# Ten loads of weights and constants move from SyncE's queue to GpSimd's, spread over tiles 0 to 5

## The reference

```python
xn = layernorm(x)
# linear attention, 16 heads of 32
Q = elu(xn @ wq.T + bq) + 1;  K = elu(xn @ wk.T + bk) + 1;  V = xn @ wv.T + bv
KV = einsum('bhsd,bhse->bhde', K, V)
out = einsum('bhsd,bhde->bhse', Q, KV) / (Q . sum_s(K) + 1e-8)
attn = out @ wo.T + bo
# gated FFN (512 -> 1376 -> 512) with a shared LoRA and 8 routed LoRA experts, top 2
gate, up = xn @ W_gate + lora + expert_lora, xn @ W_up + lora + expert_lora
ffn = (silu(gate) * up) @ W_down + lora + expert_lora
return x + attn + ffn
```

## Time and profile before

| What | Value |
|---|---|
| median of 3 runs | 675.92 us (674.55 to 676.27) |
| profiled execution: its own time | 675.29 us |
| profiled execution: span of the records | 673.5 us |
| TensorE busy | 661.8 us, 98% of the span |
| VectorE, ScalarE, GpSimd busy | 375.6, 256.3 and 126.9 us |
| granted TensorE clock | 1.00 |

### The profile page before, as it was taken

How to read it: one execution, slowest core, us unless ns; L and a number is a source line. 1 busy time by engine, 2 the same in 40 slices (tenths; PEclk the granted TensorE clock), 3 DMA queues, 4 the chain that set the end, 5 groups by cost and what they waited for, 6 DMA issues and landing times.

```text
span 673.5 us, 10336 instructions
## 1 busy us (share of the span) xinstructions
PE 661.8 (98%) x3568; PEld 544.2 (81%) x3568; DVE 375.6 (56%) x696; ACT 256.3 (38%) x412; POOL 126.9 (19%) x290
## 2 busy tenths in 40 slices
PE   7999999999999999999999999999999999999998
PEld 6889899977677788888888888888888888888886
DVE  5577788778775966344346433445444336534433
ACT  4343445467235324323233332333233314323321
POOL 3456666635256130000000000000000000000000
PEclk9999999999999999999999999999999999999999
DMA  7946566753853679940024100012400002300001
GB/s 222 328 158 225 194 202 203 249 213 150 307 218 115 253 242 3 43 161 0 0 79 169 82 0 0 0 63 78 187 0 0 0 0 78 126 0 0 0 0 62
DMA packets 40634, 74.21 MB, mean 110 GB/s; under 512 B 19280, under 2 KB 19920, under 8 KB 38688
## 3 DMA queue, kind: packets, MB, share of 16 engines
q1 hardware_dynamic: 40400, 73.56, 37.5%
q0 software_dynamic: 208, 0.30, 0.4%
HBM read 52.81 MB, written 21.04 MB: 110 GB/s over the span
## 4 chain that ended last, share of the span: by engine, by line
PE 89%; DVE 4%; issue 2%; ACT 1%; POOL 1%; DMA 1%; SPq 0%; POOLq 0%; DVEq 0%; ACTq 0%
PE bank L1196 20%; PE bank L1197 19%; PE bank L1198 19%; PE bank L1438 18%; PE bank L1411 6%; PE bank L1424 2%; DVE den L1049 1%; PE bank L1422 1%; DMA w_raw<-in_wkT 1%; PE bank L1213 1%; PE bank L1225 1%; PE bank L1311 1%; DVE qf_odd L1007 1%; PE bank L1449 1%; PE bank L1451 1%
## 5 line engine op out<-in xcount | busy, mean ns | idle before, releaser
L1196 PE MATMUL bank<-x,up_h 128*128 128x512 f32 (+1 forms) x352 | 137.1, 390 | 0.2 <-DVE x3r L1014 0.2
L1197 PE MATMUL bank<-x,up_h 128*128 128x512 f32 (+1 forms) x352 | 137.2, 390 | 0.0
L1198 PE MATMUL bank<-x,up_l 128*128 128x512 f32 (+1 forms) x352 | 137.1, 390 | 0.0
L1139 DVE TENSOR_TENSOR hf<-bank,silu 128x512 f32<-128x512 f32 x44 | 30.4, 691 | 155.4 <-issue 135.6
L1438 PE MATMUL bank<-dn,hid_h 128*128 128x512 f32 x352 | 108.7, 390 | 0.0
L660 ACT ACTIVATE hid_h<-hf 128x512 fp32r<-128x512 f32 x44 | 27.8, 632 | 142.4 <-DVE hf L1139 142.4
L1196 PEld LDWEIGHTS bank<-x,up_h 128*128 128x128 f32 x352 | 66.1, 188 | 16.5 <-issue 0.7
L1438 PEld LDWEIGHTS bank<-dn,hid_h 128*128 128x128 f32 x352 | 65.9, 188 | 14.7 <-DVE res L1158 0.6
L1197 PEld LDWEIGHTS bank<-x,up_h 128*128 128x128 f32 x352 | 66.1, 188 | 14.2
L1198 PEld LDWEIGHTS bank<-x,up_l 128*128 128x128 f32 x352 | 66.1, 188 | 13.8
L849 DVE TENSOR_TENSOR up_l<-up_raw,up_h 128x1024 fp32r<-128x1024 f32 x44 | 55.0, 1249 | 26.9 <-ACT up_h L660 26.9
(11 more groups left out here) (165 smaller groups left out, 1081.7 us busy)
## 6 DMA issues: line engine op xcount, KB each, us to landing
x<-scr_x SPq DMA_DIRECT2D x7, 2048.0 KB, 9.3
up_raw<-in_ffn_up SPq DMA_DIRECT2D x11, 768.0 KB, 7.9
scr_x<-xt SPq DMA_DIRECT2D x16, 512.0 KB, 5.3
xin<-in_x SPq DMA_DIRECT2D x16, 256.0 KB, 4.6
scr_z<-zt SPq DMA_DIRECT2D x16, 256.0 KB, 2.0
x3r<-in_x SPq DMA_DIRECT2D x16, 256.0 KB, 3.5
scr_att<-x3r SPq DMA_DIRECT2D x16, 256.0 KB, 2.7
z<-scr_z SPq DMA_DIRECT2D x4, 1024.0 KB, 4.9
```

The costliest lines, as they stand in the source:

```text
L1139: nc.vector.tensor_tensor(hf[:], ps_u[:], silu[:], ALU.mult).then_inc(h_done, 1)
L1196: nc.tensor.matmul(dst, lh, rh, start=start, stop=False, **kw)
L1197: nc.tensor.matmul(dst, lh, rl, start=False, stop=False, **kw)
L1198: return nc.tensor.matmul(dst, ll, rh, start=False, stop=stop, **kw)
```

## The change

SyncE's part loses the ten loads and the wait for `wsetl_done`. GpSimd's loop over 13 tiles becomes six written-out tiles with loads between them, and a loop from tile 6 on. There is one load behind tile 0, one behind tile 1, and two behind each of tiles 2 to 5. The sizes, the destinations, the count on `s2_in` and the wait in tile 8 stay.

```diff
@@ sync
             stage1(0, 0)
 
-            for dst, name in ((hmask, "headmask"), (hcol, "headcol"), (hrow_raw, "headrow"), (lomask, "lomask"), (bdn_raw, "b_dn"), (sb_dn, "sb_dn")):
-                sp.dma_start(dst[:], dram[name]).then_inc(s2_in, 16)
-            sp.dma_start(bv_b[:], dram["bv"]).then_inc(s2_in, 16)
-            sp.dma_start(bo_b[:], dram["bo"].to_broadcast([P, D])).then_inc(s2_in, 16)
-            sp.wait_ge(wsetl_done, 2 * KD)
-            sp.dma_start(w_raw[:, 0], dram["woT"]).then_inc(s2_in, 16)
-            sp.dma_start(w_raw[:, 1], dram["wqT"]).then_inc(s2_in, 16)
@@ gpsimd
             rstd_of(1)
             rstd_of(2)
-            with pool.Fori(0, TILES - 3) as t:
+            def load(dst, src):
+                pool.dma_start(dst, src).then_inc(s2_in, 16)
+
+            route(0)
+            pool.wait_ge(wsetl_done, 2 * KD)
+            load(w_raw[:, 1], dram["wqT"])
+            route(1)
+            load(w_raw[:, 0], dram["woT"])
+            route(2)
+            load(hmask[:], dram["headmask"])
+            load(hcol[:], dram["headcol"])
+            route(3)
+            load(bv_b[:], dram["bv"])
+            load(hrow_raw[:], dram["headrow"])
+            route(4)
+            load(lomask[:], dram["lomask"])
+            load(bdn_raw[:], dram["b_dn"])
+            route(5)
+            load(sb_dn[:], dram["sb_dn"])
+            load(bo_b[:], dram["bo"].to_broadcast([P, D]))
+            with pool.Fori(6, TILES - 3) as t:
                 route(t)
             route(TILES - 3, more=False)
```

## The result

The changed kernel takes 679.19 us (median of 7 runs, 676.93 to 680.45) against 674.94 us (7 runs, 674.55 to 676.27) for the one before: ratio 1.0054, 95% interval 1.0043 to 1.0066. By the ratio it is slower by 3.6 us (the two medians lie 4.25 us apart), where I had forecast 1.5 us faster, and it lies 0.8 us above my range.

What follows compares the result with a forecast made beforehand. TensorE was taken to bound the kernel, busy 661.8 us, 98% of the span. The terms -2.32 + 0.7 + 0.1 gave -1.5 us, so 675.92 - 1.5 = 674.4 us, range 673.2 to 678.4 us.

Steps and rivals of the forecast that it cites:

- The gain: Ten loads off SyncE's queue: tile 1's store lands earlier, ScalarE's stall in tile 3 goes, at most 2.32 us saved.
- GpSimd's lag: GpSimd issuing two loads in each of tiles 2 to 5 lengthens its tiles; 0.7 us lost after hidden time.
- c: GpSimd's added time per load between a tile's last operation and the next `rden1`; taken as 0.60 us, bounds 0.54 to 1.47.
- 4 (2c - 0.65) - 1.5: Loss in us from GpSimd's issuing over tiles 2 to 5, less a lead; 0.7 us at c = 0.60.
- the lead: How far `zst` is ready ahead of TensorE once the stall is gone; estimated 1.5 us, set against GpSimd's lag.
- the 0.65 us: Free time per tile: TensorE's 7.54 us a tile against a 6.89 us loop through GpSimd, VectorE and back.
- The round trip: From one tile's `rden1` through VectorE and GpSimd to the next tile's `rden1` and hand-over; 6.89 us without loads.
- the rival that I feared most: GpSimd is held longer per load than its queue shows, deciding at c = 0.80; 675.9 to 681.3 us, chance 0.27.
- the third, "the DMA engines": Moved 3.3 MB share the DMA engines with the stores of tiles 2 to 8; 0.1 us lost, bounds 0 and 0.6.
- the whole slack: Slack from a store to TensorE's next keys, put at 0.7 to 1.5 us, about as large as that of `zst`.
- the moved loads delay later stores: Rival: a store in tiles 4 to 8 lands 1 to 2.6 us late, ScalarE waits; 676.2 us, chance 0.10.
- The constants' wait: Wait in tile 8: the last load, issued at about 70, lands before wq is split at 78 to 80; costs nothing.

Runs made afterwards that it cites:

- act_issue: Kernel before, with the ten loads issued by ScalarE on its own queue at the end of its tiles 1 to 6; 673.10 us, ratio 0.9968.
- the two tiny kernels: sp_late and act_issue, each with ten extra 512-byte transfers issued by GpSimd at the changed kernel's places; 676.22 us and 674.14 us.
- sp_spread: Kernel before, with all ten loads still on SyncE but spread behind the stores of tiles 2 to 7; 673.19 us, ratio 0.9971.
- after_again: The changed kernel itself, measured once more; 679.96 us, ratio 1.0063 to the kernel before.
- sp_late: Kernel before, with all ten loads on SyncE in one block behind the store of tile 2; 674.92 us, ratio 0.9994.
- after_bo_plain: Changed kernel, with `bo_b` loaded from an ordinary array of 128 rows instead of one row read 128 times; 677.16 us, ratio 1.0037.
- pool_constants2: act_issue, with the eight constants issued by GpSimd and the two weights left on ScalarE; 677.06 us, ratio 1.0026 to the kernel before.
- after_last_act: Changed kernel, with the last pair, `sb_dn` and `bo_b`, issued by ScalarE behind its tile 6; 675.39 us, ratio 1.0003 to the kernel before.
- after_swap: Changed kernel, with its last two pairs of loads swapped, so `lomask` and `bdn_raw` come last; 676.37 us, ratio 1.0009 to the kernel before.
- pool_weights2: act_issue, with the two weights issued by GpSimd and the eight constants left on ScalarE; 674.50 us, ratio 0.9989 to the kernel before.
- unrolled_only: Kernel before, with GpSimd's first six tiles written out and no load moved; 674.82 us, ratio 0.9993.

## Why the prediction was wrong

**The gain** was right: -2.32 us forecast; 2.32 in those two tiles of the changed kernel, and 2.25 us of stage 1 in act_issue, where nothing takes it away. The profile looked as I had said, no wait in tile 3 and full tiles of 7.99 and 7.09 us.

**GpSimd's lag** came out about right, in part by luck: +0.7 us forecast, 0.5 to 0.6 us in stage 1 and 1.4 us by the times of the two tiny kernels. c is 0.49 (0.60 forecast), far from the 0.80 at which it would have decided, and with it the formula, 4 (2c - 0.65) - 1.5, gives -0.2, so nothing: c was too high, and the lead or the 0.65 us too large. The round trip itself was right: over two loads it is 7.8 us a tile (`rden` of the changed kernel at 55.02, 62.83 and 70.65), and 6.89 + 2 x 0.49 gives 7.87. So the rival that I feared most, with 0.27, did not come. The 1 us that the Trainium skill's page DMA: Bandwidth & Descriptors (Latency and other measured facts) gives to the first byte is not time for which GpSimd is held. As a latency this trace agrees with it better than the earlier trace rows: `sb_dn` is issued at 69.48, and the software queue's first packets are seen between 70.5 and 71.

**The step that failed is the third, "the DMA engines": 0.1 us, with 0.6 as its upper bound.** Measured, what the moved data does is 4.4 to 5.0 us (5.8 to 6.4 us of loss against act_issue, less the 1.4 us of the issues), 3.4 to 4.1 us of it by the last pair alone. What the term left out is that transfers on GpSimd's queue keep SyncE's store from landing for far longer than their bytes take. It went wrong in three ways.
- I read the room from one window, 36 to 40 us, with a share of 0.00, and called it typical. The burst with `x3a`, every second tile, fills the engines: 0.94 from 72 to 76 us in the kernel before. The last pair stands right ahead of it.
- I priced a shared transfer at its bytes over 407 GB/s. That holds for the pair on ScalarE's queue (0.9 to 1.4 us on the store, and TensorE loses nothing). Beside the software queue SyncE's moved 0.44 to 0.73 MB in the 4 us in which it moved 0.92 to 1.12 without it, and the store came 2.0 to 4.9 us later. act_issue and sp_spread move the same bytes in nearly the same tiles at no cost in time.
- I took the whole slack for the stores, though GpSimd's lag draws on it too. In after_again ScalarE starts 2.25 us late in the tile from 44.83 on (44.83 + 0.60 to 47.68), with GpSimd behind by its loads, and TensorE loses 0.74 us in the next tile. In act_issue it starts 2.22 us late in the tile from 74.39 on (to 77.21), GpSimd issues nothing, and TensorE loses nothing in that tile or the next. Both are tiles with key-value products; it is a comparison of two places, and so it fits this reading without proving it.

**The rival** "the moved loads delay later stores", with a chance of 0.10 and 676.2 us, names what happened, and so does one of the signs of being wrong ("if ScalarE's waits for `scr_x` grow"): ScalarE waits as at 33.06, for a store of tiles 4 to 8, that of tile 7. It was too small, since it too let a store come late by no more than the bytes, 2.6 us; the store in question landed 3.7 us later than before. I had looked up that GpSimd's transfers take a queue of their own kind, with packets only 4 us after the issue, and used it as a price of GpSimd's time alone, not of what it does to others.

**The constants' wait** in tile 8 cost nothing, as forecast: `wq_h` follows at 84.16, behind ScalarE's work for the late tile.

Why SyncE's transfers come so late beside GpSimd's queue, and why the engines can stand idle while both have work, is not shown by any run here. What the runs show is where the long tile comes: with `sb_dn` and `bo_b` on GpSimd's queue right ahead of the burst. Taking `bo_b`'s one-row source away shortens it, and moving the pair to another tile or to ScalarE's queue removes it. That the 1.3 us by which ScalarE's pair is earlier has no part in this is argued from sp_spread and not shown.

## What to carry to other kernels

Before loads are moved to another engine's queue, ask which kind of queue that is: spread over the tiles, these ten loads cost nothing on SyncE's or ScalarE's, and about 6 us on GpSimd's. If a block of loads delays a store, first try to spread it on the queue on which it stands; here that gave the whole 0.3%. And read the room for moved transfers from the fullest window that they will meet, not from the emptiest: one store that lands 3.7 us later than it used to took 2.9 us of TensorE's time, more than the 2.32 us stall that the change removed. And a hole in TensorE's work can cost more than its own length: twice the granted clock fell to 0.50 behind one.

## What the runs showed that I had not expected

**How late a store may be.** ScalarE's start behind the end of the transposes, and what TensorE lost in that and the next tile: 2.2 us late, nothing (act_issue at 77.21, transposes at 74.39); 3.9 late, 2.0 lost (sp_late); 4.1 late, 2.3 lost (before, tile 3); 4.3 late, 2.0 lost (after_bo_plain); 5.2 late, 2.9 lost (the changed kernel). In these five the granted clock is 1.00, about 2 us are free, and what lies beyond is paid in full. Where the clock fell behind the hole, more is paid: 6.5 late, 5.4 lost (after_again); 6.5 late, 6.5 lost (pool_constants2). And in tile 5, with the store of tile 3 late and the second weight on GpSimd's queue just ahead of it, 2.2 to 2.5 us late already cost 0.4 to 1.0 us (the changed kernel, after_again, after_bo_plain, after_last_act, after_swap, pool_weights2); pool_constants2, whose weights are ScalarE's, is 0.9 late there and loses nothing.

**The clock at the start.** Windows of the changed kernel (after the busy times: granted clock, DMA share, GB/s):

```profile
8.00:10.00 2.00, 0.23 (x3) 0.04 (x1) 0.53 (x1) 1.20 (x3) 0.33 (x1) 1.00 0.98 382
10.00:12.00 2.00, 1.19 (x3) 0.99 (x4) 2.00 (x5) 1.48 (x3) 0.00 (x0) 0.68 1.04 284
12.00:14.00 2.00, 2.00 (x7) 1.52 (x6) 1.34 (x4) 0.58 (x2) 0.45 (x2) 0.50 0.84 141
```

TensorE had been idle for most of 8 to 10 us, since the load of wk took 7.1 us to land (6.4 before), and the granted clock then fell to 0.50, the level of 1.2 GHz, just as it had work. In the kernel before it was busy for 0.93 and 1.91 us of the first two windows, and the clock stayed at 1.00.

It is tempting to take this for the 1.17 us that the profiled executions differ by ahead of stage 1, but the traces say otherwise. after_swap, whose start is that of the changed kernel, keeps a clock of 1.00 and has its first transposes at 17.70, as late as the changed kernel. act_issue and after_last_act both have them at 17.36, the first with the clock at 1.00, the second with it down at 0.50. What goes with the start is the load of wv, which landed later: first before, then the changed kernel.

```profile
w_raw<-in_wvT SPq DMA_DIRECT2D x1, 1024.0 KB, 9.5
```

```profile
w_raw<-in_wvT SPq DMA_DIRECT2D x1, 1024.0 KB, 10.8
```

ScalarE starts to split wv at 12.17 before and at 13.42 after, each time released by that load. In 12 of the 14 profiled executions the first transposes start 6.9 to 7.1 us after the figure in this row (10.8 in after_swap, 10.4 in act_issue and after_last_act). SyncE's program is the same up to there in all of them, and the figure goes from 7.9 (unrolled_only) to 11.0 (after_again), so one profile of before can't tell whether the change has a part in it.

The mean granted clock of a whole execution was below 0.998 in 11 of the 12 executions of the changed kernel that list it, and in 22 of 83 of the kernel before; in after_swap it was in 1 of 11. So the fall is more frequent in the changed kernel. In the kernel before, executions at 0.997 took 0.3 to 0.7 us more than those at 1.00, and so the ratio holds some tenths of a us of it. How many of the falls lie at the start and how many behind the long tile, the executions without a profile don't tell.
